# Three triangle layers and a scan layer on one core: spread products a step later, first decays from PSUM, x added in the first bank

## What is computed

```python
xn = _ln(x, norm_scale, norm_bias)
left = (xn @ Wl + bl) * mask * sigmoid(xn @ Wlg + blg)
right = (xn @ Wr + br) * mask * sigmoid(xn @ Wrg + brg)
out_gate = sigmoid(xn @ Wog + bog)
out = _banded_ingoing(left, right, 4)     # 9 shifted products along one axis
out = _ln(out, out_norm_scale, out_norm_bias) * out_gate
x = x + (out @ Wo + bo)                   # the x given to the layer is _gn(x)
...
x, z = split(xs @ W_in)                   # the scan layer: 256 rows long, 64 channels
xc = silu(conv4(x)); dt_r, B, C = split(xc @ W_x)
dt = softplus(dt_r @ W_dt + b_dt)
h = exp(dt * A) * h + dt * B * xc;  y = sum over 16 states of h * C
x = x + (((y + xc * D) * silu(z)) @ W_out)
```

## Time and profile before

| what | value |
|---|---|
| time, median of 3 runs | 2915.89 us (2911.53 to 2921.84) |
| the profiled execution | 2918.08 us, its span 2916.3 us |
| mean granted clock | 0.942 |
| busy share PE, DVE, ACT, POOL | 81%, 80%, 64%, 70% |
| triangle layers 0, 1, 2 with the hand-over | to 407, 407 to 810, 810 to 1221 us (first half of a layer overlaps the end of the one before) |
| scan layer | 1221 to 2916 us |

### The profile page before, as it was taken

The page is one execution under the profiler, slowest core; times in us unless marked ns, Lnnn a source line. Parts: engine busy times, 40 slices in busy tenths (PEclk is TensorE's granted clock), DMA queues, the critical chain, the costliest instruction groups (busy, mean ns, idle before and its releaser), DMA issues.

```text
span 2916.3 us, 37812 instructions
## 1 busy us (share of the span) xinstructions
PE 2360.2 (81%) x13018; PEld 741.1 (25%) x13018; DVE 2325.2 (80%) x2039; ACT 1853.9 (64%) x2534; POOL 2052.0 (70%) x1194
## 2 busy tenths in 40 slices
PE   4889878898888977478788887888878788787886
PEld 1233122441224421122222222222222222222221
DVE  5655566655565544389999999999999999999997
ACT  3624656245562434377778777777877778777773
POOL 2544244542445422269999999999999999999998
PEclk9999999999998988789999999999999999999997
DMA  4798316983159845676777767767777776767774
GB/s 162 244 328 247 106 45 211 342 275 108 52 183 343 276 136 149 134 178 169 185 176 180 188 166 187 177 175 183 174 188 172 184 178 177 189 165 188 177 176 113
DMA packets 257980, 538.30 MB, mean 185 GB/s; under 512 B 39624, under 2 KB 150992, under 8 KB 256896
## 3 DMA queue, kind: packets, MB, share of 16 engines
q1 hardware_dynamic: 230896, 469.09, 59.2%
q0 software_dynamic: 19040, 64.24, 7.5%
q10 hardware_dynamic: 7856, 2.56, 0.4%
HBM read 396.46 MB, written 139.33 MB: 184 GB/s over the span
## 4 chain that ended last, share of the span: by engine, by line
DVE 24%; issue 16%; ACT 9%; PE 7%; POOL 1%; DMA 0%; ACTq 0%; DVEq 0%; SPq 0%; POOLq 0%
DVE m_hs L473 13%; DVE m_pb L468 12%; ACT m_da L410 4%; PE m_pb L304 2%; ACT L366 1%; ACT m_act L358 1%; ACT L352 1%; PE m_py L284 1%; PE m_misc L242 1%; PE m_py L277 1%; ACT m_act L364 1%; POOL m_hs L486 1%; DMA m_dtb<-dt_rows 0%; PE m_misc L234 0%; PE m_misc L265 0%
## 5 line engine op out<-in xcount | busy, mean ns | idle before, releaser
L486 POOL TENSOR_TENSOR m_hs<-m_hs,m_cs 128x1024 f32<-128x1024 f32 x512 | 1200.4, 2359 | 130.2 <-DVE m_hs L473 80.2
L473 DVE TENSOR_TENSOR_SCAN m_hs<-m_da,m_pb 128x1024 f32<-128x1024 f32 x416 | 951.3, 2287 | 19.1 <-ACT m_da L410 4.7
L304 PE MATMUL m_pb<-m_dtx,late 64*128 64x512 f32 x1664 | 502.3, 677 | 233.7 <-DVE m_hs L473 226.2
L468 DVE TENSOR_TENSOR m_pb<-m_pb,m_bs 128x1024 f32<-128x1024 f32 x416 | 502.8, 1209 | 9.2 <-PE m_pb L304 9.0
L410 ACT ACTIVATE m_da<-m_dtb,m_a_neg 128x1020 f32<-128x1020 f32 x416 | 466.5, 1143 | 3.5 <-DMA m_dtb<-dt_rows 1.3
L1484 POOL TENSOR_TENSOR t_xc<-t_xc,big 128x512 f32<-128x512 f32 x96 | 120.2, 1270 | 333.2 <-DVE big L1390 333.0
L304 PEld LDWEIGHTS m_pb<-m_dtx,late 64*128 64x128 f32 x1664 | 155.3, 200 | 555.6 <-DVE m_hs L473 320.1
L284 PE MATMUL m_py<-m_hs,late 128*32 128x512 f32 x2048 | 277.0, 613 | 7.3 <-POOL m_hs L486 7.3
L1362 DVE SCALAR_TENSOR_TENSOR t_xc<-t_bank,t_vec,t_xc 128x512 f32<-128x512 f32 x96 | 72.0, 750 | 244.2 <-PE t_bank L1052 244.2
L1247 ACT ACTIVATE t_sq<-t_bank 128x512 f32<-128x512 f32 x192 | 106.9, 598 | 227.3 <-PE t_bank L1091 227.1
L1481 POOL TENSOR_TENSOR t_sq<-big 128x512 f32<-128x512 f32 x96 | 102.9, 1082 | 186.2 <-ACT big L1229 109.2
(11 more groups left out here) (160 smaller groups left out, 3847.0 us busy)
## 6 DMA issues: line engine op xcount, KB each, us to landing
m_dtb<-dt_rows SPq DMA_DIRECT2D x512, 512.0 KB, 5.7
late<-right_factor POOLq DMA_DIRECT2D x102, 512.0 KB, 6.2
right_factor<-t_tile SPq DMA_DIRECT2D x192, 256.0 KB, 3.9
t_tile<-band_out SPq DMA_DIRECT2D x183, 256.0 KB, 4.1
band_out<-t_vwin SPq DMA_DIRECT2D x48, 512.0 KB
band_out<-t_vwin SPq DMA_DIRECT2D x48, 480.0 KB
dt_rows<-m_dt SPq DMA_DIRECT2D x64, 256.0 KB, 4.6
t_xc<-in_x_cm SPq DMA_DIRECT2D x4, 2048.0 KB, 14.5
```

The lines of the kernel that those rows point to most:

```text
L304: m = nc.tensor.matmul(pb[s % 2][:, half(n)], spread[rows, dg, :], dtx[par][rows, half(q)], start=True, stop=True)
L468: nc.vector.tensor_tensor(products, products, bs[q][:, :], ALU.mult).then_inc(u_done, 1)
L473: nc.vector.tensor_tensor_scan(hs[:, g % H_RING, :], decays, products, 0.0, ALU.mult, ALU.add).then_inc(h_ready, 1)
L486: nc.gpsimd.tensor_tensor(hs[:, g % H_RING, :], hs[:, g % H_RING, :], cs[q][:, :], ALU.mult).then_inc(hc_ready, 1)
```

## The change

It has three parts. In the triangle layers `bc3` is planned one step later, and within its step it is done early on PE and DVE; a table `LOADS` replaces the rule for the loads, and units 14 and 15 are loaded in steps 58 and 60 (before 60 and 61); ACT opens the gates of unit 0 ahead of its squares; and four hand-over DMAs of SP go to ACT's queue, with a wait for the second group of x stores alone. In the scan layer's begin, two extra matmuls are ahead of the first convolution, z of chunk 0 is computed within chunk 0, xg of chunk 1 too, and the first two steps' decays are read from PSUM, where two new pairs of matmuls spread dt, instead of from DRAM. At its end the sums go into bank `py[0]`, x is added and the first half projected ahead of the last sum.

```diff
@@ plan()
-                    steps[at]["bc3"] += [n, n + 1]
+                    steps[at + 1]["bc3"] += [n, n + 1]
...
+        LOADS = [[] for _ in STEPS]
+        for n in A3:
+            LOADS[A3_STEP[n] - {14: 3, 15: 2}.get(n, 1)].append(n)
@@ SP
-                        for n in STEPS[s + 1]["a3"] if s + 1 < len(STEPS) else ():
+                        for n in LOADS[s]:
                             load_out(l, n)
...
-                hand_over(sp, first_row(16, 1), 8 * 28)
                 sp.wait_ge(x_stored[3], 16 * 4 * 4)
                 hand_over(sp, first_row(28, 0), first_row(16, 1))
@@ PE, in a step
                         for n in st["a3"]:
                             project(l, "og", n, w_og, 4, flip=1)
+                        for n in st["bc3"]:
+                            rows, i = rstd_rows(l, "root3", n)
...
+                            nc.tensor.matmul(bank[b][:, :], sel3[cg:cg + 64, i // 2, :], rows[cg:cg + 64, :],
+                                             start=True, stop=True).then_inc(full[b], 1)
+                        for n in st["a3"]:
                             for p in range(2):
                                 wait_bank(p, (l, "c3", n, p))
...
-                        for n in st["bc3"]:     (the same, behind the bands)
@@ ACT
+                            if n == 0 or n >= LATE:
                                 open_gates(l, n)
...
+                a.wait_ge(x_stored[1], 16 * 4 * 8)
+                hand_over(a, first_row(16, 1), first_row(24, 1))
                 a.wait_ge(x_stored[3], 16 * 4 * 4)
-                hand_over(a, 8 * 28, ROWS)
+                hand_over(a, first_row(24, 1), ROWS)
@@ DVE, in a step
+                        for n in st["bc3"]:
+                            b = bc3_bank(n)
+                            v.wait_ge(full[b], use[l, "bc3", n])
+                            v.wait_ge(free[2], use[l, "y1", n])
+                            nc.vector.tensor_tensor(xn_unit(n), xn_unit(n), bank[b][:, :], ALU.mult).then_inc(free[b], 1)
                         for n in st["y2"]:
...
-                        for n in st["bc3"]:     (the same, behind the bands)
@@ scan layer, ACT
+                def first_decay(s):
+                    a.wait_ge(dt_spread, s + 1)
+                    for n in range(2):
+                        rows = py[n][:, :].rearrange("p (r t) -> p r t", t=T)[:, :, 1:T]
+                        m = nc.scalar.activation(da[:, s, SUB * n:SUB * n + SUB, 1:T], rows, ACT.Exp, scale=a_neg[:, DGS[s]:DGS[s] + 1])
+                    m.then_inc(da_ready, 1)
@@ scan layer, PE, the drain and post of the last chunk
-                        for late in range(S + 1 - LAG, S, 2):
-                            sum_two(k - 1, 1 - par, late)
+                        late = range(S + 1 - LAG, S, 2)
+                        sum_two(k - 1, 1 - par, late[0])
+                        pe.wait_ge(y_taken, 2 * k - 1)
+                        add_x(k - 1, 0)
+                        pe.wait_ge(y_gated, 2 * k - 1)
+                        project_out(0, 0)
+                        for two in late[1:]:
+                            sum_two(k - 1, 1 - par, two)
...
+                    if k == CHUNKS - 1:
+                        project_out(1, 0).then_inc(o_ready, 1)
+                        return
```

More of the change, by code:

```diff
@@ L227, in pre @@
                         q = int(op[1])
+                        for _ in range(2) if early(k, 1) and q == 0 else ():
+                            nc.tensor.matmul(pb[1][:, 0:HALF], eye[:, :], spread[:, 0:4, :].rearrange("p a b -> p (a b)"), start=True, stop=True)
                         pe.wait_ge(xg_ready, 2 * k + q + 1)
@@ L236, in pre @@
                         m.then_inc(misc_ready[q], 1)
-                    elif op == "z":
+                    elif op[:9] == "spread dt":
+                        s = int(op[10:])
+                        if s == 0:
+                            pe.wait_ge(misc_used[0], use(0, "dt") + 1)
+                        else:
+                            pe.wait_ge(da_ready, s)
+                        for n in range(2):
+                            rows = slice(D * n, D * n + D)
+                            m = nc.tensor.matmul(py[n][:, :], spread[rows, DGS[s], :], dt[rows, half(0)], start=True, stop=True)
+                        m.then_inc(dt_spread, 1)
+                    elif op in ("z", "z first"):
                         for q in range(2):
@@ L350, in pre @@
                         m.then_inc(xg_ready, 1)
+                    elif op == "silu x":
+                        for q in range(2):
+                            a.wait_ge(misc_ready[q], use(k, "x") + 1)
+                            nc.scalar.activation(act[par][:, half(q)], misc[q][:, :], ACT.Silu,
+                                                 bias=conv_b).then_inc(misc_used[q], 1)
+                    elif op == "tables":
+                        a.preload_act_table_set("natural_log_exp_and_others")
+                    elif op == "first decays":
+                        for s in range(2):
+                            first_decay(s)
                     elif op == "silu":
@@ L416, in steps @@
                 def steps(k, par, s, first, last):
-                    for t in ([0, 1] if first and s == 0 else []) + decays_of(s):
+                    for t in ([], [2, 3])[s] if first and s < 2 else decays_of(s):
                         if t < S:
@@ L786, in numbering @@
                         fill(band_bank(t), (l, "band", t))
-                    for n in st["bc3"]:
-                        fill(bc3_bank(n), (l, "bc3", n))
                     for b in st["root1"]:
@@ L1126, in _ @@
                             band(l, t)
-                        for n in st["bc3"]:
-                            rows, i = rstd_rows(l, "root3", n)
-                            cg = 64 * (i % 2)
-                            b = bc3_bank(n)
-                            wait_bank(b, (l, "bc3", n))
-                            nc.tensor.matmul(bank[b][:, :], sel3[cg:cg + 64, i // 2, :], rows[cg:cg + 64, :],
-                                             start=True, stop=True).then_inc(full[b], 1)
             @block.scalar
```

89 lines of the change are left out of this document (58 added, 31 removed).

## The result

Over all rounds the changed kernel takes 2894.87 us in the median (2886.04 to 2906.11, 7 runs) where the kernel before takes 2917.07 (2911.53 to 2921.84, 7 runs); the ratio is 0.9927, with a 95% interval of 0.9907 to 0.9948. So it is faster, by 22 us, where 52 had been forecast, and it lies outside the range. The profiled execution has a span of 2891.3 us, 25.0 less than before.

The account below looks back on a forecast made before the run. The prediction saw layer 2's PE waiting for loads behind x stores, then running slowly. Terms -48 + 6.4 - 1 - 5.9 - 3.7 = -52.2 us from 2918.08 gave 2865.9, as median 2863.7; range 2848 to 2888.

Parts of the forecast that it names:

- the root steps: Triangle layers, steps where ACT loads tables for roots: spreading matmuls move to the next step, +2.1 us at each of two.
- DVE's products ahead of its x addition: Triangle layers' bc3 steps: the new order on DVE costs nothing, since PE's 2.19 us of spreading stand ahead of centring matmuls.
- layer 2, from the end of layer 1 to the variance matmuls: Layer 2: loads issued ahead of waiting x stores recover most of the 60.8 us excess over layer 1, -48 us.
- layers 0 and 1: First two triangle layers: root steps and layer ends cost more than earlier loads and gates gain, +3.2 us each, +6.4.
- 12.8 left as not recovered: Layer 2: unit 12's load 3, unit 16 2, contention 3, excess before the stores 3.5, root steps 1.3 us.
- the split: Hand-over: four of SP's eight DMAs go early to ACT, halving SP's 9.65 us of issue less late landings, -3.8 us.
- rival (d): Hand-over: splitting gives nothing because the DMAs share engines, +3 instead of -1 us, 2867.7 in all; chance 0.2.
- S + 11.2: Scan layer's begin: first scan 11.2 us after S, the end of the second silu of x; before, S + 18.5.
- give-back in the begin: Scan layer's chunk 0: ACT waits and lost DVE time by scans 8 to 10 return 2.4 us of the gain.
- (a): Layer 2: the stalls only move, gain some 20 us instead of 48, about 2892 in all; chance 0.12.
- (b): Triangle layers: layer 2 becomes a layer 1, -57 us, and the roots hide, about 2848 in all; chance 0.15.
- (c): Triangle layers: DVE's pair ahead of its x addition delays centring matmuls, 1.27 us in 48 steps, about 2925; chance 0.04.

Follow-up runs that it names:

- third experiment: The changed kernel with only PE's spreading matmuls moved ahead of the variance matmuls of the same step; 2879.16 us, ratio 0.9863 to the kernel before.
- second experiment: The kernel before with the scan layer's begin and end changes, and SP storing x units one step later; 2869.3 us, ratio 0.9835.

## Why the prediction was wrong

**The step that failed** is the price of the root steps and of the new place of the spreading on PE: "For the roots ... these matmuls go to the next step: +2.1 each", and "PE fills that gap in part" as all that hangs on it. I had seen the cover, and priced its loss only for two roots a layer, and had one of them given back by the layer's end. And I priced DVE's products ahead of its x addition at nothing.

What the runs show in its place: the cover is lost at three roots (the one of units 8 to 13 too), where the variance matmuls wait 2.60, 2.75 and 2.69 us for the squares in layer 0 (306.18, 349.31, 382.27), and the DVE products make the output matmuls wait in nearly each bc3 step, since the odd unit's spreading uses bank 3, which the prediction did not name. Layers 0 and 1 grew by 7.1 and 6.6 us instead of 3.2, about 2.3 of it ahead of the variance matmuls of units 30 and 31 (forecast 0.5) and 4.6 behind them. Putting the matmuls back ahead, with nothing else, gives 19 us by the ratios, of the 30 that were missing.

**The terms beside each other,** forecast and measured:

| term | forecast | measured |
|---|---|---|
| layer 2, from the end of layer 1 to the variance matmuls | -48 | -42.1 |
| layers 0 and 1 | +6.4 | +13.8 |
| from there to the barrier (last x units, hand-over) | -1 | +11.4 |
| begin of the scan layer and its chunks | -5.9 | -4.3 |
| end | -3.7 | -3.8 |
| sum | -52.2 | -25.0 |

By its trace the third experiment, which moves the spreading alone, wins 5.1 and 4.9 us in layers 0 and 1, 5.6 in layer 2 up to the variance matmuls and 4.3 behind them, 19.9 of the 27.2 us that are missing in this table. What is left lies between those matmuls and the barrier: in the third experiment too that stretch is 7.3 us longer than before, against the forecast's -1.

**Layer 2.** The -42.1 is -28.3 less the 13.8 by which layer 1 ended later. The mechanism, loads ahead of waiting stores, was right: without the new waits, in the second and in the third experiment, the stretch falls by 47.6 (374.2 us in both). That this comes so near to 48 is partly luck, since the 12.8 left as not recovered was a sum of guesses, and the load waits there stay at 20.3. Behind the variance matmuls, the tail to the last statistics was forecast at +3 and is +8.9: 1195.80 to 1207.72 was 11.9 us, 1167.51 to 1188.32 is 20.8. Of this 4.7 is what layer 0's end lost too (391.45 to 402.24, and 393.87 to 409.38). The rest has a wait of its own: POOL waited 6.70 us in its own queue ahead of a hand-over DMA, for x stores. SP issues 40 of them in one row (the row below is cut at 1190 by its window):

```profile
1162.50 27.66 SPq L979 DMA_DIRECT2D x_layer<-t_xc  x37
...
1168.10 1.28 POOL L1557 TENSOR_TENSOR t_xc<-t_xc,big 128x512 f32<-128x512 f32 x1
1176.08 1.05 POOL L923 DMA_DIRECT2D big<-x_layer  x1 [6.70 <-issue]
```

That POOL waits there for SP's stores is by the code (`x_stored[1]`) and these rows; no run took it away. Before, POOL had such a wait too, 9.25 us until 1190.92, but then stood idle for DVE for 4.53 us more, so it cost nothing there. In the second experiment, where only the stores come later, the wait is 5.30 us and the tail is 16.6 us (1147.48 to 1164.11), 4.7 more than before, while layer 0's tail is as before (389.47 to 400.26, 10.8). So the later stores lengthen the last tail by themselves, which the prediction had only as +3 for later x units.

**The hand-over** was -3.8 for the split and is +2.5: the sign was wrong. ACT's queue of twelve takes 14.64 us where SP's and ACT's eight took 9.65 and 12.02 side by side, and the four DMAs that SP keeps are done 6 us ahead. The last x stores land 2.6 us later behind the statistics than before, and with SP's eight DMAs back the trace wins 2.8.

The Trainium skill, "DMA: Bandwidth & Descriptors", "Issuing engines are not separate DMA queues", says that spreading issues over engines saves sequencer time alone; I had weighed it as rival (d). Nothing in the traces speaks against it, but they don't tell issue time from transfer time either. In eight kernels the barrier opens 0.75 to 0.78 us behind the last issue. Yet the last issues take up to 2.5 us each where the first take 0.34, and in 1189 to 1196 of the changed kernel the DMA engines are 0.92 busy, so the transfers may be what holds the issues up.

**Right:** the begin (-5.9 forecast, -4.9 measured; first scan at S + 11.2, measured S + 10.95), and the end (-3.7, -3.8). In the end the high clock came, for which the prediction had up to 4.4; the half of the projection that is left takes 1.07 us, no less than half of the old 1.98. The give-back in the begin had its size off, 2.4 forecast and 3.9 measured, and it had come by scan 6, not at scans 8 to 10. The extra matmuls, forecast at 1.0, are worth 1.1 at scan 20.

**Rivals:** (a) was nearest by its time, 2892, but that is luck: the load waits in layer 2 did fall. (b) did not come: layer 1 is longer than 371.76, not shorter. (c) names DVE's product ahead of the x addition; its waits came on the output matmuls, not the centring ones, and were 0.28 to 2.48 us a time. PE's cover which I gave for it is where the argument broke: the matmuls of the spreading are ahead of the centring matmuls, but what follows them is the y2 sum, and that waits for their reader.

The Trainium skill, "PSUM — Partial Sum Buffer", section "PSUM bank collisions raise a hardware error", asks that accesses of two engines to one bank be guarded by semaphores. This kernel has such guards on bank 3, and the traces give the price: each wait of the output matmuls, 0.28 to 2.48 us, ends with DVE's product, which reads that bank.

## What to carry to other kernels

Before a piece of work is moved, ask what wait it fills where it stands: four matmuls of 2.2 us between two dependent steps were free there, and when they went, the wait that they had filled grew from at most 0.7 us to 2.6 us and more. When a change helps by reordering one queue, try that queue's order alone; here SP's order gave 38 us, and all of the triangle changes together 11 to 14. A PSUM bank shared by two users puts the reader of the first in the way of the second, so list every user of the bank when its place in the order changes.

## Not expected of the hardware

The same triangle program varies between executions by several microseconds a layer: layer 0 ended at 409.38 and at 414.74 in two kernels with the same code up to there, and layer 2 of the second experiment took 390.8 us where that of the same kernel with the loads and the gates took 401.6. Yet that one is the faster kernel by its median; its profiled execution is the slowest of its five. So a trace's difference of 5 us in a layer needs a named wait behind it.
